# Attention over 4096 positions with float32 products split in two: g from 256-column products with its bias folded into the last shift, and diagonal score chunks computed from the diagonal on

## The reference, cut to what matters

```
x: (4, 256, 64, 64) float32; v = groupnorm(x), 32 groups of 8 channels
g = g_w v + g_b                      # (b, 128, 4096)
f = v^T v                            # (b, 4096, 4096), symmetric
y = softmax(f, axis=-1) g^T          # (b, 4096, 128)
wy = W_w y^T + W_b                   # (b, 256, 4096)
wy = (wy - mean) * rsqrt(var + 1e-5) * gamma + beta     # over batch and positions
out = x + wy + v
```

## Time and profile before

| what | value |
|---|---|
| median of 3 runs | 2267.2 us (2264.66 to 2268.2) |
| profiled execution, its own time | 2274.37 us |
| its span | 2272.3 us |
| PE, busy share | 94% |
| DVE, ACT, POOL, busy share | 66%, 48%, 36% |
| mean granted TensorE clock | 0.984 |

### The profile page before, as it was taken

The page is one execution under the profiler, slowest core; times in us unless marked ns, Lnnn a source line. Parts: engine busy times, 40 slices in busy tenths (PEclk is TensorE's granted clock), DMA queues, the critical chain, the costliest instruction groups (busy, mean ns, idle before and its releaser), DMA issues.

```text
span 2272.3 us, 32522 instructions
## 1 busy us (share of the span) xinstructions
PE 2138.1 (94%) x9520; PEld 1522.6 (67%) x9520; DVE 1509.5 (66%) x3062; ACT 1095.2 (48%) x2234; POOL 811.3 (36%) x624
## 2 busy tenths in 40 slices
PE   5899999999999999999999999999999999999988
PEld 4787776665687776665678677665668777666433
DVE  5566666776755766686756666677765676667556
ACT  3344444556444445447444444545644445454645
POOL 3002122559501023347730122345950202345650
PEclk9999999999999999999999999999999999999999
DMA  3112233445512223454521223344551232246879
GB/s 135 75 75 86 95 113 125 163 146 165 181 44 84 100 90 112 144 185 133 192 76 76 79 102 112 125 162 149 174 169 43 88 116 89 93 137 206 304 256 360
DMA packets 108407, 304.55 MB, mean 134 GB/s; under 512 B 11456, under 2 KB 11968, under 8 KB 93888
## 3 DMA queue, kind: packets, MB, share of 16 engines
q1 hardware_dynamic: 108224, 302.37, 38.8%
HBM read 159.71 MB, written 142.61 MB: 133 GB/s over the span
## 4 chain that ended last, share of the span: by engine, by line
PE 67%; POOL 12%; issue 11%; ACT 4%; DVE 3%; DMA 2%; SPq 0%; DVEq 0%; POOLq 0%; ACTq 0%
PE bank L1183 10%; PE bank L1124 10%; PE bank L1126 9%; PE bank L1125 9%; PE bank L1159 8%; POOL fy_d L690 4%; PE bank L1187 4%; PE bank L1189 4%; PE bank L1188 4%; POOL fy_c L690 4%; PE bank L1324 3%; ACT ring L756 2%; PE bank L1254 2%; POOL xl L663 2%; DVE plo L961 1%
## 5 line engine op out<-in xcount | busy, mean ns | idle before, releaser
L782 ACT CAST phi<-bank 128x512 fp32r<-128x512 f32 x480 | 280.6, 586 | 818.8 <-PE bank L1159 818.1
L926 DVE TENSOR_SCALAR_CACHE_REDUCE ring<-bank 128x512 f32<-128x512 f32 x576 | 396.5, 688 | 290.9 <-PE bank L1126 287.4
L1124 PE MATMUL bank<-xh 128*128 128x512 f32 x1152 | 542.0, 471 | 7.2 <-POOL xl L663 6.4
L1126 PE MATMUL bank<-xh,xl 128*128 128x512 f32 x1152 | 457.3, 397 | 0.0
L1125 PE MATMUL bank<-xl,xh 128*128 128x512 f32 x1152 | 454.3, 394 | 0.0
L961 DVE TENSOR_TENSOR plo<-bank,phi 128x512 fp32r<-128x512 f32 x480 | 325.9, 684 | 165.9 <-ACT phi L782 121.8
L1159 PEld LDWEIGHTS bank<-ident,ring 128*128 128x128 f32 x1920 | 234.9, 143 | 201.5 <-issue 131.7
L1159 PE MATMUL bank<-ident,ring 128*128 128x128 f32 x1920 | 296.6, 278 | 60.7 <-ACT ring L756 29.6
L756 ACT ACTIVATE ring<-ring,nmax 128x512 f32<-128x512 f32 x480 | 344.7, 720 | 0.0
L690 POOL TENSOR_TENSOR fy_c<-fy_c,maxrow 128x512 f32<-128x512 f32 x200 | 261.8, 1312 | 159.6 <-DMA fy_c<-spill 159.6
L690 POOL TENSOR_TENSOR fy_d<-fy_d,maxrow 128x512 f32<-128x512 f32 x188 | 241.6, 1288 | 184.0 <-DMA fy_d<-spill 184.0
(11 more groups left out here) (110 smaller groups left out, 2784.0 us busy)
## 6 DMA issues: line engine op xcount, KB each, us to landing
spill<-ring SPq DMA_DIRECT2D x112, 1024.0 KB, 4.4
fy_c<-spill SPq DMA_DIRECT2D x200, 256.0 KB, 4.6
fy_d<-spill SPq DMA_DIRECT2D x188, 256.0 KB, 4.1
ring<-x_dram SPq DMA_DIRECT2D x40, 512.0 KB, 4.6
lbuf<-spill SPq DMA_DIRECT2D x60, 256.0 KB, 3.7
yd<-yn SPq DMA_DIRECT2D x32, 256.0 KB, 3.3
fx_a<-x_dram SPq DMA_DIRECT2D x16, 512.0 KB, 8.3
out_dram<-fx_a SPq DMA_DIRECT2D x16, 512.0 KB, 4.5
```

Source lines behind the costliest of these rows:

```text
L926: last = nc.vector.tensor_scalar(ring[:, SLOT[u], t, :], src, 1.0, None, ALU.mult, ALU.max, accum_out=rowm[:, t, c:c + 1])
L1124: nc.tensor.matmul(dst, xh[:, k, rows], xh[:, k, cols], start=(k == 0), stop=False)
L1126: last = nc.tensor.matmul(dst, xl[:, k, rows], xh[:, k, cols], start=False, stop=(k == K - 1))
```

## The change

Three things are changed. (1) In a diagonal chunk, product t computes only the columns from t*128 on: 512, 384, 256 and 128 columns. The t tiles left of the diagonal are transposes of what was already taken for the rows above, out of `ring` into the same PSUM bank, so that `take_f` finds a full 128x512 result. For that `multiply` waits, behind its six matmuls, for the take of the product directly before it. (2) `make_g` handles half a chunk (two tiles) at a time. The high and low parts of the weights lie side by side in `wgs`, so that one matmul of 256 columns gives high*high and high*low next to each other. Per tile it issues two of 256 columns and two of 128 columns. DVE's `add_g` sums the two column blocks with a reduction, twice per chunk. (3) The bias of g no longer enters g. Because the weights of the softmax sum to one, it adds a constant W_w g_b to wy, which is computed once near the end (two small matmuls into `sps`) and added to W_b in `wbias`.

```diff
-G_AT = {T * (c - 1) - 1: c for c in range(2, NB)}
+G_AT = {T * (c - 1) - 2 + h: (c, h) for c in range(2, NB) for h in range(2)}
...
-NEXT_G_AT = {TILES - 16 + 4 * c: c for c in range(2)}
+NEXT_G = range(2)
+NEXT_G_AT = {TILES - 16 + 4 * c + h: (c, h) for c in NEXT_G for h in range(2)}
...
-        wgh = sb("wgh", [P, K, CI], F32R)
-        wgl = sb("wgl", [P, K, CI], F32R)
+        wgs = sb("wgs", [P, K, 2 * CI], F32R)
+        wgh, wgl = wgs[:, :, 0:CI], wgs[:, :, CI:2 * CI]
...
-            def add_bias(n, c, first=False):
-
-                dve.wait_ge(g_made, n * NB + c + 1)
-                nc.vector.tensor_tensor(gf[:, c, :, :], sps.rearrange("p (t c) -> p t c", t=T),
-                                        bgb[:, :].unsqueeze(1).broadcast_to([P, T, CI]), ALU.add).then_inc(g_added, 1)
+            def add_g(n, c, h):
+
+                dve.wait_ge(g_made, n * (2 * NB) + 2 * c + h + 1)
+                nc.vector.tensor_reduce(gf[:, c, 2 * h:2 * h + 2, :], sps.rearrange("p (t o c) -> p t c o", t=T // 2, o=2),
+                                        AX.X, ALU.add).then_inc(g_added, 1)
...
+            dve.wait_ge(bias_made, 1)
+            nc.vector.tensor_tensor(wbias[:, :], sps[:, 0:2 * K].rearrange("p (k o) -> p k o", o=2)[:, :, 0],
+                                    vecs[:, 0, :], ALU.add).then_inc(bias_taken, 1)
             dve.wait_ge(wy_counted, B * K * NB)
...
                 rows = slice(j * W + t * P, j * W + (t + 1) * P)
-                cols = slice(c * W, (c + 1) * W)
-                dst = fps[:, s % 2, :]
+                own = t * P if c == j else 0
+                cols = slice(c * W + own, (c + 1) * W)
+                dst = fps[:, s % 2, own:]
...
+                if own:
+
+                    pe.wait_ge(f_taken, n * NPROD + s)
+                    for above in range(t):
+                        last = nc.tensor.transpose(fps[:, s % 2, above * P:(above + 1) * P],
+                                                   ring[:, SLOT[CHUNK_NO[j, c]], above, own:own + P], ident[:, :])
                 last.then_inc(f_made, 1)
 
-            def make_g(b, c, first=False):
+            def make_g(b, c, h, first=False):
...
-                for r in range(T):
+                for r in range(2 * h, 2 * h + 2):
                     rows = slice(c * W + r * P, c * W + (r + 1) * P)
-                    dst = sps[:, r * CI:(r + 1) * CI]
+                    both = sps[:, r % 2 * 2 * CI:(r % 2 + 1) * 2 * CI]
+                    high = sps[:, r % 2 * 2 * CI:r % 2 * 2 * CI + CI]
+                    nc.tensor.matmul(both, xh[:, 0, rows], wgs[:, 0, :], start=True, stop=False)
                     for k in range(K):
-                        nc.tensor.matmul(dst, xh[:, k, rows], wgh[:, k, :], start=(k == 0), stop=False)
-                        nc.tensor.matmul(dst, xh[:, k, rows], wgl[:, k, :], start=False, stop=False)
-                        last = nc.tensor.matmul(dst, xl[:, k, rows], wgh[:, k, :], start=False, stop=(k == K - 1))
+                        nc.tensor.matmul(high, xl[:, k, rows], wgs[:, k, 0:CI], start=False, stop=False)
+                    last = nc.tensor.matmul(both, xh[:, 1, rows], wgs[:, 1, :], start=False, stop=True)
                 last.then_inc(g_made, 1)
...
+            pe.wait_ge(wy_counted, B * K * NB)
+            for k in range(K):
+                last = nc.tensor.matmul(sps[:, 2 * k:2 * k + 2], wwt[:, k * P:(k + 1) * P], bgc[:, :],
+                                        start=True, stop=True)
+            last.then_inc(bias_made, 1)
```

More of the change, by code:

```diff
@@ L671, in image @@
             def image(b, more):
-                for c in range(len(NEXT_G_AT), NB):
+                for c in range(len(NEXT_G), NB):
                     make_gl(b, c)
@@ L679, in image @@
                             make_xl(b + 1, c)
-                    for s, c in NEXT_G_AT.items():
-                        if more and w == AHEAD[s]:
+                    for s, (c, h) in NEXT_G_AT.items():
+                        if more and h == 1 and w == AHEAD[s]:
                             make_gl(b + 1, c)
@@ L710, in _ @@
                 make_xl(0, c)
-            for c in NEXT_G_AT.values():
+            for c in NEXT_G:
                 make_gl(0, c)
@@ L1052, in _ @@
             merge_max(0, 0)
-            add_bias(0, 0, first=True)
-            add_bias(0, 1, first=True)
+            for c in NEXT_G:
+                for h in range(2):
+                    add_g(0, c, h)
             for p in range(HEAD):
@@ L1296, in _ @@
             pe.wait_ge(wg_lo, 1)
-            for c in NEXT_G_AT.values():
-                make_g(0, c, first=True)
+            for c in NEXT_G:
+                for h in range(2):
+                    make_g(0, c, h, first=True)
             for p in range(LAG):
```

59 lines of the change are left out of this document (32 added, 27 removed).

## The result

| | before | after |
|---|---|---|
| median of timed executions | 2266.38 us (4 runs, 2264.66 to 2268.20) | 2228.12 us (4 runs, 2227.25 to 2233.52) |
| profiled execution, its span | 2274.37, 2272.3 us | 2227.25, 2225.5 us |

The ratio is 0.9828, with an interval of 0.9808 to 0.9849: 38 us faster, where 46 were forecast. The profiled executions differ by 47 us, so the first question is which of the two numbers is the change's.

The account below looks back on a forecast made before the run. PE's own stream was taken to bound the kernel (busy 94%). 32.5 - 4 + 24.0 - 0.35 - 0.5 - 0.9 = 50.8 us, less 5 absorbed, leaves 46: from 2267.2 to 2221 us, range 2208 to 2243.

Parts of the forecast that it names:

- Bound: Whole kernel: PE's own pace sets the time nearly everywhere; a microsecond out of PE's stream is worth close to one.
- Diagonal, -32.5: 32 diagonal chunks: narrowed products save 53.4 us, 192 added transposes cost 20.9, net 32.5 us (24.0 to 34.4 between bounds).
- streaming plus 15 ns: Matmul price in the diagonal chunks: streaming time plus a fixed 15 ns, so 0.122 us at 256 columns, 0.175 at 384.
- rival of dear widths: 256 and 384 columns cost 0.151 and 0.190 us, time 2237; chance 0.22, shared with more absorption (2233 to 2260).
- the prologue: Before the first loop: g's halves lose 0.35 us uncovered, and the first diagonal chunk's saving counts 0.5 us less.
- New wait, +4: Transposes wait for the preceding take: 1.05 us in images 1 to 3, 0.2 in image 4, 0.7 in first (0,0); sum 4.
- g, -24.0: g blocks of 24 matmuls become 8 of 256 and 8 of 128 columns: 0.80 us in each of 30 chunks, 24.0 us.
- Bias at the end, +0.9: Kernel's end: two small float32 matmuls and a DVE add between last statistic and aggregation cost 0.9 us.
- Absorbed, 5: Stage 5, chunks (7,7) and (0,0): PE waits for left tiles from POOL, ACT and DVE; 5 of 7 us saved are lost.
- Clock: Whole run: mean granted clock 0.984, some 36 us lost at half speed; a gain in microseconds carries over, clock 0.98 or above.
- rival that 14 more stretches come: Half-clock stretches of 6.8 us cost 3.4 us each, so 14 undo 46 us; 2330 if one per diagonal chunk; chance 0.03.
- Doing nothing: Products and transposes balance out at 2267; transposes would have to cost 0.28 us each; chance 0.02.

Follow-up runs that it names:

- g only: Kernel after with whole 512-column products in the diagonal chunks (no transposes), so g in half blocks and the moved bias alone; 2246.23 us, ratio 0.9894 to before.

## Why the prediction came out right

The time, 2228, lies in the range and 7 us above the forecast of 2221; without the clock's part the gain is 44 to 46 us, where 46 were forecast. The large terms were right in mechanism and size; that the small ones add up so well is in part luck, as the steps show:

- **Bound.** Right for stages 0 to 4 and the largest part of the time: there what left PE's stream became time nearly one for one. "Nearly everywhere" was too much: stage 5 keeps most of a saving, and stage 6 and the tail don't get longer when PE runs at half clock, so 115 of the 540 us of each of images 1 to 3, and the tail, are paced by something else. Of the 57.0 us that left PE's stream (by counts times distances, against 56.5 in the sum) 44 to 46 came out as time.
- **Diagonal, -32.5.** The prices of 384 and 256 columns that no row showed were inside the bounds and within 2 ns of the values taken; streaming plus 15 ns held. The rival of dear widths is out. Alone, the part gave 22.8 to 24.5 us by its profile and 28.7 by its timed executions without the clock; its terms of the sum, with the wait, the prologue and what is absorbed, make 23.0.
- **New wait, +4.** The sum was right (3.7), and by luck, since the places were only half right. In (7,7) it is 0.7 an image, not 1.05, and in the first (0,0) 0.17, not 0.7. At step 3 it was not foreseen: I had written that everywhere else 0.4 us or more was to spare, and counted takes as they lay before, not behind the new reduction. Without any wait the stages show 4.6 us less, so it costs about 1 us more than the idle time in front of the transposes.
- **g, -24.0.** Right: 0.93 us for a half block, and DVE's 18 us more are hidden as said. g only, with its share of the prologue and the bias in it, came to 20.6 by its timed executions and 23.3 to 24.4 by its profile, where the terms make 22.7. That moving halves a step later delays POOL's `gl` and costs 1 us in each of three images was missed; it had no term in the sum.
- **Bias at the end, +0.9.** 1.15 in the profile; alone, too small to be told from none (1.0004).
- **Absorbed, 5.** Stage 5 kept 1.7 to 2.0 us in each of three images and is within 0.3 us as long as without the saving. That was the most uncertain term, and right in size and place; its reason, that POOL, ACT and DVE deliver the left tiles late, was not shown (above).
- **Clock.** I said that a gain in microseconds carries over. It does not quite: the low level of the clock took 6 to 8 us of it. The rival that 14 more stretches come is out (the low level is 81.5 us instead of 76.0 in the profiled executions). By the mean clock, 0.003 lower, the timed executions have an estimated 13 us more of it, about two of the longer stretches, and that is what stands between 46 and 38 if all of it costs. Charging every stretch with half its length, as the rival and the 36 us lost before did, is itself too much, by what stage 6 and the tail show.
- **Doing nothing.** This rival's condition was worked out for the diagonal chunks alone: 53.4 us over 192 transposes are the 0.28 each. With g's 24 us it would have needed 0.40. The measured 0.110 excludes both.

## What to carry to other kernels

Where 128-column matmuls follow each other with a new weight each, count the matmuls with their loads, not the columns: joining two products of the same stationary tile in one wider matmul costs almost nothing for the second. A dependency on the instruction just before is cheap only if that instruction is not queued behind something else on its engine; look at the order on the other engine after the change, not before. When a few microseconds are in question and the granted clock varies, set the clock's part aside first, or medians of parts will not add up; and look whether a slow stretch lies in a stage that PE paces, since elsewhere it costs nothing.

## What was not expected of the hardware

The start of stage 6 ran at 1.2 GHz in one kernel and at 2.4 in another, behind the same pause (above). And two small writes of DVE at an address that comes from a register lasted long; its timeline of after, image 3:

```profile
1526.44 1.10 DVE L901 TENSOR_TENSOR gnp<-gst 128x2 f32 x1 [0.21 <-POOL gst L661]
...
1527.46 0.15 DVE L903 SCALAR_TENSOR_TENSOR gst<-gst 128x2 f32<-128x2 f32 x1
1527.53 1.25 DVE L905 TENSOR_SCALAR gnp<-gst 128x2 f32 x1
```

1.10 and 1.25 us for 128x2 elements, where one of the same size to a fixed address between them takes 0.15. In the prologue, where the image's number is a constant, the same two lines take 0.16 us each, which speaks for the register. It is not shown, though: a write of four columns to a fixed address (`nmax`, 0.17 us in 28 of 32 cases) took 0.56 us three times and 1.20 once in after, and over 1 us four times in before.
